# Issuing the transfers of P V's outputs from ACT behind its copy, with the inversion of the softmax sums standing further back

## What is computed

```python
x = x + ga * attn(layernorm(x) * (1 + ca) + sa)
x = x + gb * ffn(layernorm(x) * (1 + cb) + sb)

# attn
q, k, v = split(x @ qkv_w.T)                  # 16 heads of 16
scores = einsum('bhqd,bhkd->bhqk', q, k) * scale
probs = softmax(scores)
out = einsum('bhqk,bhkd->bhqd', probs, v)     # heads side by side
out = out @ proj_w.T + proj_b
```

## Time and profile before

| | |
|---|---|
| median of 3 runs | 1084.84 us (1083.93 to 1085.31) |
| the profiled execution | 1084.72 us |
| its span in the trace | 1082.8 us |
| mean granted TensorE clock | 0.956 |
| PE busy | 1015.1 us, 94% |
| DVE busy | 781.8 us, 72% |
| ACT busy | 644.4 us, 60% |
| POOL busy | 229.8 us, 21% |

### The profile page before, as it was taken

How to read it: one execution, slowest core, us unless ns; L and a number is a source line. 1 busy time by engine, 2 the same in 40 slices (tenths; PEclk the granted TensorE clock), 3 DMA queues, 4 the chain that set the end, 5 groups by cost and what they waited for, 6 DMA issues and landing times.

```text
span 1082.8 us, 16389 instructions
## 1 busy us (share of the span) xinstructions
PE 1015.1 (94%) x5784; PEld 503.4 (46%) x5784; DVE 781.8 (72%) x1540; ACT 644.4 (60%) x1260; POOL 229.8 (21%) x348
## 2 busy tenths in 40 slices
PE   5999999999988899999999999999999999999977
PEld 2453333334434454544444445554444555453555
DVE  3877888888867687777877887777787667784143
ACT  2127677777766466666658676666567456556610
POOL 3400123005143130001434230001443000151000
PEclk8959899999998899999999999999999999998989
DMA  6803141515130410425330514008230500320001
GB/s 161 162 1 50 36 82 33 71 42 118 27 49 17 84 28 12 70 41 128 80 46 23 78 32 70 12 18 151 73 53 12 79 7 10 84 68 12 11 1 45
DMA packets 53214, 58.83 MB, mean 54 GB/s; under 512 B 21431, under 2 KB 41404, under 8 KB 53120
## 3 DMA queue, kind: packets, MB, share of 16 engines
q1 hardware_dynamic: 52332, 56.92, 27.1%
q0 software_dynamic: 384, 0.79, 0.4%
q10 hardware_dynamic: 416, 0.08, 0.0%
HBM read 23.16 MB, written 4.47 MB: 26 GB/s over the span
## 4 chain that ended last, share of the span: by engine, by line
PE 73%; DVE 8%; SPq 6%; ACT 5%; DMA 3%; issue 3%; POOL 1%; ACTq 0%; DVEq 0%
PE pE L747 22%; PE pX L747 20%; PE pO L747 19%; PE pM L747 10%; DVE mx L1174 3%; SPq L1666 3%; DMA orow<-osb 2%; SPq L1680 2%; SPq L1682 1%; ACT P L1051 1%; ACT hi L1101 1%; ACT h1T L1085 1%; DVE lo L1260 1%; ACT h2f L1128 1%; DVE Hb L1327 1%
## 5 line engine op out<-in xcount | busy, mean ns | idle before, releaser
L1174 DVE TENSOR_REDUCE mx<-pM 128x1 f32<-128x512 f32 x1006 | 630.0, 682 | 116.9 <-PE pM L747 113.3
L1051 ACT ACTIVATE P<-pE 128x512 f32<-128x512 f32 x996 | 527.2, 599 | 244.2 <-PE pE L747 240.9
L747 PE MATMUL pM<-KO,QO 48*128 48x512 f32 x1006 | 375.5, 463 | 23.5 <-DVE mx L1174 21.3
L747 PE MATMUL pE<-QO,KO 50*128 50x512 f32 x996 | 354.7, 445 | 10.2 <-ACT h2f L1128 2.7
L747 PEld LDWEIGHTS pE<-QO,KO 50*128 50x128 f32 x996 | 168.9, 191 | 235.2 <-issue 134.4
L747 PE MATMUL pO<-P,V 128*17 128x512 f32 x2048 | 262.4, 610 | 0.7 <-ACT P L1051 0.6
L747 PEld LDWEIGHTS pM<-KO,QO 48*128 48x128 f32 x1006 | 168.6, 192 | 59.3 <-DVE mx L1174 49.3
L1507 POOL CAST mh<-mxc 128x16 fp32r<-128x16 f32 x32 | 6.5, 202 | 417.2 <-DVE mxc L1183 417.1
L747 PEld LDWEIGHTS pO<-P,V 128*17 128x17 f32 x2048 | 41.4, 96 | 103.0 <-issue 93.7
L747 PE MATMUL pX<-h1T,wqkv_s 128*128 128x512 f32 x112 | 60.1, 645 | 1.7 <-DVE lo L1260 1.5
L747 PE MATMUL pX<-X,Hb 128*128 128x258 f32 x216 | 56.9, 401 | 0.8 <-DVE Hb L1327 0.2
(11 more groups left out here) (293 smaller groups left out, 929.2 us busy)
## 6 DMA issues: line engine op xcount, KB each, us to landing
KO<-hi SPq DMA_DIRECT2D x56, 128.0 KB, 4.0
QO<-hi SPq DMA_DIRECT2D x56, 128.0 KB, 5.2
x<-in_x SPq DMA_DIRECT2D x20, 256.0 KB, 3.2
out<-x SPq DMA_DIRECT2D x16, 256.0 KB, 2.3
AT<-osb SPq DMA_DIRECT2D x124, 32.0 KB, 2.0
asum<-sums SPq DMA_DIRECT2D x124, 32.0 KB, 1.9
KO<-lo SPq DMA_DIRECT2D x28, 128.0 KB, 3.8
QO<-lo SPq DMA_DIRECT2D x28, 128.0 KB, 5.6
```

The costliest lines, as they stand in the source:

```text
L747: return e.matmul(o, lhsT, rhs, start=start, stop=stop)
L1051: e.activation(P[:, u % 3, j, :], bank(s), ACT.Exp).then_inc(*empties(s))
L1174: e.tensor_reduce(mx[:, hq % 2, k:k + 1, kh], bank(s), AX.X, ALU.max, negate=True).then_inc(*empties(s))
```

## The change

The step `oput` is gone. Its eight DMAs are issued by ACT, right behind its copy of `pO` and ahead of every later exponential in ACT's list. The four of the sums now go first and the four of the outputs behind them, where before they took turns. ACT waits for its own copy, for the projections of the batch before that read the same columns of `AT` (only those of this half, `proj` 2c+1, where SP waited for `proj` 3), and for the sums of the piece before to have left `orow`. The distances for `orec` and `oget` in the plan are new: `orec` stands 2.3 units behind the last `PV` of its piece (before: 0.6 for `oput` and 1 more), `oget` 0.8 behind it (before 1).

```diff
-    if kind == "oput":
-        return [(("gates", 8), 0), (("PV", 8 * b + 7), 0.6)]
     if kind == "orec":
-        return [(("oput", b), 1)]
+        return [(("PV", 8 * b + 7), 2.3)]
     if kind == "oget":
-        return [(("orec", b), 1)]
+        return [(("orec", b), 0.8)]
...
-            waiting["quiet"][:0] = [("oput", hq), ("orec", hq), ("oget", hq)]
+            waiting["quiet"][:0] = [("orec", hq), ("oget", hq)]
...
                     e.activation(osb[:, :], pO[:, :], ACT.Copy).then_inc(s_osb, 1)
+                    if s[1] < NU - 1:
+                        gi, c = SEQ[hq]
+                        b, g = divmod(gi, 4)
+                        act.wait_ge(s_osb, hq + 1)
+                        act.wait_ge(s_gates, 1)
+                        if b:
+                            act.wait_ge(*full("proj", b - 1, 2 * c + 1))
+                        if hq:
+                            act.wait_ge(d_sums, 16 * hq)
+                        for j in range(4):
+                            e.dma_start(orow[32 * j:32 * j + 32, :],
+                                        osb[32 * j + HD:32 * j + HD + 1, :]).then_inc(d_orow, 16)
+                        for j in range(4):
+                            p0 = 64 * (g % 2) + HD * j
+                            e.dma_start(AT[p0:p0 + HD, g // 2, 512 * c:512 * c + 512],
+                                        osb[32 * j:32 * j + HD, :]).then_inc(d_put[c], 16)
...
-                elif kind == "oput":
-                    hq = s[1]
-                    gi, c = SEQ[hq]
-                    b, g = divmod(gi, 4)
-                    sp.wait_ge(s_gates, 1)
-                    sp.wait_ge(s_osb, hq + 1)
-                    if b:
-                        sp.wait_ge(*full("proj", b - 1, 3))
-                    if hq:
-                        sp.wait_ge(d_sums, 16 * hq)
-                    for j in range(4):
-                        p0 = 64 * (g % 2) + HD * j
-                        e.dma_start(AT[p0:p0 + HD, g // 2, 512 * c:512 * c + 512],
-                                    osb[32 * j:32 * j + HD, :]).then_inc(d_put[c], 16)
-                        e.dma_start(orow[32 * j:32 * j + 32, :], osb[32 * j + HD:32 * j + HD + 1, :]).then_inc(d_orow, 16)
```

More of the change, by code:

```diff
@@ L33 @@
 SHORT = {"ln1turn", "mturn", "oturn", "atturn", "xturn", "select", "modT2"}
-QUIET = {"oput", "orec", "oget", "onorm", "wbload", "gates", "ln1load", "ln1s", "ln1n", "prep", "prepb", "xload", "addx", "bn2", "ln2s", "ln2n", "xsq", "xhi", "wsplit", "wload", "scale", "pick", "fetch"}
+QUIET = {"orec", "oget", "onorm", "wbload", "gates", "ln1load", "ln1s", "ln1n", "prep", "prepb", "xload", "addx", "bn2", "ln2s", "ln2n", "xsq", "xhi", "wsplit", "wload", "scale", "pick", "fetch"}
 BURST = 3
@@ L328, in weigh @@
             b, g = divmod(SEQ[hq][0], 4)
-            waiting["quiet"][:0] = [("oput", hq), ("orec", hq), ("oget", hq)]
+            waiting["quiet"][:0] = [("orec", hq), ("oget", hq)]
             if hq == parts(b, g // 2, SEQ[hq][1])[-1]:
-                waiting["quiet"].insert(3, ("onorm", b, g // 2, SEQ[hq][1]))
+                waiting["quiet"].insert(2, ("onorm", b, g // 2, SEQ[hq][1]))
     credit, at, pv = 0.0, 0, 0
```

## The result

The changed kernel takes 1250.41 us in the median (1247.21 to 1259.68, 4 runs), the kernel before in the same comparison 1084.38 (1083.11 to 1085.31, 4 runs). The ratio is 1.155, 95% interval 1.148 to 1.161. Forecast were 1260 us, with a range of 1150 to 1325.

A forecast was written before the change was run, and what follows sets the result against it. PE, working 94% of the span, was taken as the bound. 1084.7 us, less 22 of gain at `orow`, plus 113 of pauses and 84 of slow clock, gave 1260 us, with a range of 1150 to 1325.

The forecast's parts named there:

- The pauses: Behind ACT's 31 copies, eight issues delay the exponentials by 5.1 us, so PE's score matmuls wait for a bank: 113 us.
- The clock's share: Each of PE's 31 pauses brings a stretch at half clock, 6.8 us long with 0.4 of it lost: 84 us.
- The gain at orow: DVE's waits for the sums in `orow` nearly vanish, saving PE 13 us of idle time and 9.5 of slow clock: 22 us.
- Pauses without the clock's share: PE waits behind ACT's issues as forecast but its clock stays up: 1176 us, chance 0.15.
- The issues don't hold the exponentials: The second rival: ACT finishes its eight issues before PE needs a bank, leaving only the gain: 1063 us, chance 0.06.
- ACT and SP hinder each other: Issues on ACT take longer while SP issues its copies, 0.8 us each, pauses 43 us more: 1303 us, chance 0.08.

The follow-up runs named there:

- fill: The changed kernel, with PE doing 12 extra matmuls of a constant in each pause, ahead of the waiting score matmul; 1215.17 us, ratio 1.120 to the kernel before.
- sp_at_pv: The changed kernel with its new order, but SP issues the eight transfers at the last `PV` unit, sums first; 1068.27 us, ratio 0.985 to the kernel before.
- early_sp: The kernel before with its list of steps, but SP issues the transfers at the last `PV` unit, sums first; 1062.97 us, ratio 0.980.
- hold8: The kernel before, nothing moved, plus eight extra DMA issues of unread data on ACT behind each of its first 31 copies; 1254.07 us, ratio 1.155.
- late_orec: The kernel before, SP still issuing at `oput`, with only the inversion of the sums (`orec`, `oget`) moved to its new place; 1084.97 us, ratio 1.000.
- spread: The changed kernel with the same eight issues on ACT, one behind each of the next eight exponentials; 1060.85 us, ratio 0.977 to the kernel before.
- act_at_oput: The kernel before, list of steps unchanged, but ACT instead of SP issues the eight transfers at step `oput`, sums first; 1176.53 us, ratio 1.085.

## Why the prediction was right, step by step

- **The pauses (113 us forecast, for all 31 copies).** The mechanism is right; the size was 15 us too low. The row of waits gives 113.2 us in 31 places, but that agreement is chance. All 31 pauses together are 128.5 us, 16.5 of them at pieces 8, 9, 16 and 19 in other rows. I had looked only for the score matmul that needs the first bank. At pieces 16 and 19 what PE needs first is `h2f` and `h1T`, which also stand behind the issues in ACT's list. ACT's absence (forecast 5.1 us) is 5.09 at its shortest, 5.10 in the median and 5.31 in the mean. The price of an issue was bounded from both sides by the two on ACT (0.52 apart) and the 248 on SP. To go by the same transfers and not by the same engine was right: the medians on ACT are 0.611 and 0.612.
- **The clock's share (84 us less 9.5).** The mechanism is shown by fill; the size was 21 us too large. The time at 0.50 can be worked out from the mean clocks, (1 - 0.956) x 2 x 1082.8 = 95 us before and (1 - 0.895) x 2 x 1245.4 = 262 after. I had 31 x 6.8 less 23.8 = 187 us more, and it is 166. Of these, 34 fall into times in which PE has nothing in work (41.6 us in the trace of after, 7.2 in that of before, by the clock's record laid over PE's instructions) and cost nothing; at piece 5 it is 2.2 us. The other 132 us cost 53.8 us of busy time, a factor of 0.41, so the 0.4 that I had used was right. (Some 4 us of the 53.8 are not the clock's: a burst behind a pause takes 1.70 us at 0.50 where others take 1.58, as its matmuls follow ACT's pace.) What I left out is that a slow stretch can begin within its own pause.
- **The gain at orow (22 us).** By itself it is real, 17 us in sp_at_pv and 22 in early_sp, and DVE no longer waits for `orow`. But it does not add up with the pauses. hold8, which has the pauses and not the gain, takes 1254 us, the changed kernel 1250, and their executions overlap. In hold8 two thirds of DVE's wait vanish with the transfers issued as before, and PE's wait for the maxima falls from 21.3 to 10.5 us. I take it that PE's pauses let DVE reach the inversion later; no run tests that. The wait was 34.9 us before, and in hold8:

```profile
DVE orow L1201 <- DMA orow<-osb: 12.4, 3, 10.1
```

- **The sum.** Forecast were 113 of pauses, 74.5 of the clock net of the 9.5, and 13 less of waiting for the maxima, 175 us in all. Measured are 128.5, 53.8 and 19.3, which give 163.0, and the span grew by 162.6. So nothing of weight is left over, and that the sum came out only some 10 us too high is in part luck: pauses 15 too low against a clock term 21 too high.
- **Later place of the inversion.** I gave it no price of its own. late_orec shows that it is worth nothing alone, and early_sp, without it, is not slower than sp_at_pv is with it.
- **Rivals.** *Pauses without the clock's share* (1176 us) falls with the measured clock and fill. *The issues don't hold the exponentials* falls with hold8. *ACT and SP hinder each other*: some issues on ACT are longer (up to 2.1 us), but the mean absence is 0.22 us above the shortest, 7 us over all 31 pieces, where this rival had 43.

The Trainium skill, "DMA: Bandwidth & Descriptors", section "Issuing engines are not separate DMA queues", says that issuing from several engines saves only the sequencer's time to initiate, which is usually small against the DMA. For one transfer here it is 0.61 us against a landing 1.8 to 2.0 us behind the issue, so a third and not nothing, and eight in one go take 5.0 us of ACT's time. hold8 shows that this time costs 168 us, so the second rival, which I had tied to that page, does not hold.

## What to carry to other kernels

A DMA issue is an instruction in its engine's list, here of 0.6 us, and several in one go take that engine away from whoever needs it. Before moving them to an engine that is busy 60% of the time, don't go by that share. Read at the place itself how long its consumers can go on without it: how many buffers are full, and when anything that it makes is next asked for. If it must be that engine, put one issue behind each of its own instructions. The same 248 issues cost 166 us in one go, and as spread they give the lowest median here, 1060.85 us against 1085.3 (early_sp, with SP as the issuer, is within the intervals of it).

## What the runs showed of the hardware that I had not expected

- An issue on ACT runs beside the activation ahead of it in the list if it need not wait for its result: in spread the two start 0.02 us apart, and the pair takes 0.64 us. The price of an issue depends on what stands ahead of it, 0.15 us behind an exponential of 0.6 us and 0.63 in a row of issues.
- A stretch at the slow clock can begin before a long pause is over (250.8 against 253.04 at piece 5), so the pause pays for part of it. At piece 18 it begins at 721.83, behind the pause's end at 721.42.
- Behind the pause of 1.78 us at piece 23 the slow clock didn't come at all. The length of one pause does not settle it, though: behind the 1.85 us at piece 7 of act_at_oput (over at 303.50) it came:

```profile
301.60:305.10 3.50, 1.65 (x11) 0.69 (x14) 0.07 (x1) 2.25 (x5) 0.00 (x0) 1.00 0.15 35
305.20:308.50 3.30, 3.30 (x18) 0.62 (x12) 2.53 (x5) 1.27 (x3) 0.00 (x0) 0.50 0.00 0
```
